# Two scatter tables in place of four in the first layer of a graph network kernel

## The chip, the cores and the metric

The kernel runs on one core of a Trainium2 chip. The metric is the device time of one execution in microseconds (us). Each time below that is not called a median comes from one profiled execution.

## The reference

A graph has 8192 nodes with 128 features each and 262144 edges, sorted by `dst`. Two layers follow each other, and each is added to its input and normalized over the 128 features.

```
def layer0(x, src, dst, weight, W):
    gathered = x[dst] * weight[:, None]
    return segment_sum(gathered, src, 8192) @ W.T
def layer1(x, src, dst, attr, w0..w4):
    summand = tensor_product(x[src], attr, w0..w4)
    return segment_sum(summand, dst, 8192) / sqrt(10)
x = layernorm(x + layer0(x, src, dst, edge_weight, W))
x = layernorm(x + layer1(x, src, dst, edge_attr_9, w0..w4))
```

The change touches only layer 0 and the first norm. In layer 0 the rows that are read lie close together, since `dst` is sorted, but the rows that are added to (`src`) are spread at random over the nodes.

## The kernel before

The program is written by hand for each engine, with semaphores and loops. It has five stages: `setup` (index arithmetic and zero fill), `layer0`, `norm0`, `layer1`, `norm1`. A stage ends with a barrier of all engines, so what one stage gives back is not overlapped by the next.

Layer 0 treats the edges in 2048 tiles of 128 edges, in halves of 8 tiles. For a half, TensorE (PE) fetches the node rows by matmuls with one-hot matrices, ScalarE (ACT) multiplies them by the edge weights into `msg`, PE sums the messages of edges of a tile that have the same `src` (`added`), and ACT copies the sums into one of 16 slots of `sums`, two tiles in a copy (L490). VectorE (DVE) works out the row numbers `row_no` (`rows_of`, L537 to L547). Then GpSimd (POOL) issues one indirect DMA for each tile (L640), which adds 128 rows of 512 bytes to a table in DRAM.

An accumulating DMA reads its rows and writes them later, so two of them on the same table must not overlap. The kernel keeps `TABLES = 4` tables, each with its own semaphore `table_add[k]`, and lets tile t go to table t modulo 4. Before each issue POOL waits until the last DMA on that table has ended, and then tells ACT by the semaphore `turns` that one more slot is free:

```
k = t % TABLES
use = n * (H // TABLES) + t // TABLES
if t == 0:
    pool.wait_ge(rows_known, n + 2)
pool.wait_ge(table_add[k], use * 16 + 16)
pool.sem_inc(turns, 1)
```

The tables are zeroed by `fill` (L178): three in `setup`, the last one after the first windows of `x` have been asked for. `norm0` loads the four tables and `x` in 16 batches of 512 rows (L706, L708); POOL adds the four tables in three adds (L718, L719, L721); PE transposes and multiplies by `W`; DVE and ACT normalize; ACT stores. `norm1` is the same routine without tables.

Of the kernel before, what the change touches and what calls it, by code (L numbers as in the profile page):

```python
# [29 lines left out]
ALU = mybir.AluOpType  # L30
# [11 lines left out]
HALF_TILES = 8  # L42
QUAD_TILES = 4
ROW_EDGES = ROW_TILES * P
TABLES = 4
ZERO_CUTS = 4
EPS = 1e-5
NEIGHBORS = 10.0
# [74 lines left out]
def gnn_kernel(nc, x, src, dst, attr, weight, w_lin, w_tp, consts, out, tables, x1):  # L123
# [8 lines left out]
    with ExitStack() as ctx:  # L132
        def sb(name, shape, dt):
            return ctx.enter_context(nc.sbuf_tensor(name, shape, dt))
# [18 lines left out]
        g.row_start = sb("row_start", [P, g.RN], I32)  # L153
        g.table_add = [ctx.enter_context(nc.semaphore(f"table_add{k}")) for k in range(TABLES)]
        with ExitStack() as mid:
# [5 lines left out]
            setup(nc, g, src, dst, weight, w_lin, consts, tables)  # L161
            layer0(nc, g, x, tables, w_tp)
        norm_stage(nc, g, "norm0", x, x1, tables)
        layer1(nc, g, x1, attr)
        norm_stage(nc, g, "norm1", x1, out, None)

# [7 lines left out]
def fill(pool, g, tables, k):  # L175

    n_zero = (g.N + P) // ZERO_CUTS
    pool.dma_start(tables[k].rearrange("n d -> (n d)").rearrange("(p c f) -> p c f", p=P, c=ZERO_CUTS),  # L178
                   g.acc[:, 0:n_zero].unsqueeze(1).to_broadcast([P, ZERO_CUTS, n_zero])
                   ).then_inc(g.table_add[k], 16)  # L180

def setup(nc, g, src, dst, weight, w_lin, consts, tables):

    RN, TN = g.RN, g.TN
    with ExitStack() as ctx:
# [45 lines left out]
        def _(pool):  # L232
            pool.wait_ge(zeroed, 1)
            for k in range(TABLES - 1):
                fill(pool, g, tables, k)
# [111 lines left out]
def layer0(nc, g, x, tables, w_tp):  # L347
# [4 lines left out]
    with ExitStack() as ctx:  # L352
# [52 lines left out]
        def passes(eng):  # L405

            return eng.Fori(0, eng.value_load(g.n_pass[0:1, 0:1], min_val=1, max_val=g.PASSES0))
# [215 lines left out]
        def _(pool):  # L623
            pool.wait_ge(windows_asked, 1)
            fill(pool, g, tables, TABLES - 1)

            pool.sem_inc(turns, 2 * H - TABLES)
            with passes(pool) as w:
                with pool.Fori(0, RN) as r:  # L630
                    for h in range(2):
                        n = (w * RN + r) * 2 + h
                        for t in range(H):
# [3 lines that stand above are left out]
# [13 lines left out]
SLOTS = 4  # L650

def norm_stage(nc, g, name, x_in, x_out, tables):
# [3 lines left out]
    with ExitStack() as ctx:  # L657
        def sb(n, shape, dt):
            return ctx.enter_context(nc.sbuf_tensor(f"{name}_{n}", shape, dt))

        def sem(n):
            return ctx.enter_context(nc.semaphore(f"{name}_{n}"))
# [3 lines left out]
        tab_t = [[sb(f"t{i}_{k}", [P, BATCH, D], F32) for k in range(n_in - 1)] for i in range(SLOTS)]  # L666
# [11 lines left out]
        loaded = [sem(f"loaded{i}") for i in range(SLOTS)]  # L678
        free = sem("free")
        tab_sum = sem("tab_sum")  # L680
        pool_step = sem("pool_step")
        pre_made = sem("pre_made")
        feat_made = sem("feat_made")
        y_made = sem("y_made")
# [13 lines left out]
        @block.sync  # L698
        def _(sp):
            sp.sem_inc(free, SLOTS)  # L700
            with sp.Fori(0, NB // SLOTS) as i:  # L701
                for s in range(SLOTS):
                    b = i * SLOTS + s
                    sp.wait_ge(free, b + 1)
                    for k in range(n_in - 1):
                        sp.dma_start(tab_t[s][k][:], tiles(tables[k][0:g.N, :])[bass.ds(b, 1)].squeeze(0)  # L706
                                     ).then_inc(loaded[s], 16)
                    sp.dma_start(x_t[s][:], tiles(x_in)[bass.ds(b, 1)].squeeze(0)).then_inc(loaded[s], 16)  # L708

        @block.gpsimd  # L710
        def _(pool):
            if tables:
                assert len(tables) == 4
                with pool.Fori(0, NB // SLOTS) as i:
                    for s in range(SLOTS):
                        t0, t1, t2, t3 = [t[:] for t in tab_t[s]]
                        pool.wait_ge(loaded[s], i * (16 * n_in) + 16 * n_in)
                        nc.gpsimd.tensor_tensor(t0, t0, t1, ALU.add).then_inc(pool_step, 1)  # L718
                        nc.gpsimd.tensor_tensor(t2, t2, t3, ALU.add).then_inc(pool_step, 1)  # L719
                        pool.wait_ge(pool_step, i * (2 * SLOTS) + (2 * s + 2))  # L720
                        nc.gpsimd.tensor_tensor(t0, t0, t2, ALU.add).then_inc(tab_sum, 1)  # L721
            else:
                pool.sem_inc(y_made, 2)
                with pool.Fori(0, NB // 2) as i:
                    for s in range(2):
                        b = i * 2 + s
                        pool.wait_ge(y_made, b + 1)
                        nc.gpsimd.tensor_copy(feat[s][:], g.acc[:, bass.ds(b * (BATCH * P), BATCH * P)].rearrange(
                            "f (p a) -> f a p", a=BATCH)).then_inc(feat_made, 1)
# [367 lines left out]
```

## Time and profile before

| | before |
|---|---|
| median of 3 runs | 7495.48 us (7493.65 to 7499.33) |
| profiled execution, span from first to last instruction | 7497.9 us |
| setup and first windows | 0 to 61.8 us |
| layer 0, first to last scatter-add issue | 61.85 to 3853.23 us |
| norm0 | about 3861 to 3949 us |
| layer 1 | about 3949 to 7437 us |
| norm1 | about 7437 to 7498 us |
| POOL busy over the span | 69% |
| PE busy over the span | 57% |
| mean granted TensorE clock | 0.666 of full speed |

The profiled execution has no time of its own beside its span; the span lies 2.4 us above the median of the runs. In a row of the groups of instructions, the first number behind the bar is busy time in us and the second the mean duration in ns. In a row of the timeline the first number is the start in us and the second how long the row lasts; the bracket tells how long the engine had been idle and what released it. A releaser `issue` means that nothing in the profile was waited for.

### The profile page before, as it was taken

The page shows a single profiled execution, that of the slowest core. Times are in us where ns is not written, and L with a number is a line of the kernel's source. Part 1 is how long each engine was busy: PE and PEld are TensorE (multiplying, and loading weights), DVE is VectorE, ACT ScalarE, POOL GpSimd, SP SyncE. Part 2 cuts the span into 40 slices and gives each one's busy share as a digit, 9 for nine tenths or more (in the row PEclk, how much of TensorE's full clock was granted, in tenths as well). Part 3 has the DMA queues.
Part 4 walks back from the last instruction along what each step waited for, and adds up shares of the span by engine and source line. Part 5 has one row for each costly group of instructions (what it writes and reads, how often), then busy time and mean ns, then how long its engine had stood idle before and what let it go on. Part 6 is the DMA issues. An engine that isn't in the chain of part 4 may idle for free. (4 is left out here: it accounts for less than half of the span.)

```text
span 7497.9 us, 88065 instructions
## 1 busy us (share of the span) xinstructions
PE 4281.0 (57%) x20579; PEld 3387.1 (45%) x20709; DVE 2007.2 (27%) x4415; ACT 1277.5 (17%) x3653; POOL 5183.9 (69%) x4168
## 2 busy tenths in 40 slices
PE   5555555556555555556545556555555665555555
PEld 4444444444444444444434445444444554444444
DVE  4222222222222222222242222222222222222224
ACT  2222222222222222222221000000000000000002
POOL 5888888888888888888875555555555555555554
PEclk7666666666667667666666665766766656676665
DMA  5444444444444444444451111111111111111112
GB/s 137 40 40 40 40 40 40 40 40 40 40 40 40 40 40 40 40 40 40 40 149 47 42 41 41 41 41 41 42 42 42 41 41 41 41 42 42 42 42 69
DMA packets 423293, 349.11 MB, mean 47 GB/s; under 512 B 74464, under 2 KB 369632, under 8 KB 420848
## 3 DMA queue, kind: packets, MB, share of 16 engines
q0 software_dynamic: 362560, 285.74, 27.8%
q1 hardware_dynamic: 56112, 54.84, 2.4%
q10 hardware_dynamic: 4608, 8.39, 0.3%
q14 instruction: 9, 0.07, 0.0%
q8 instruction: 4, 0.07, 0.0%
HBM read 189.03 MB, written 159.65 MB: 47 GB/s over the span
## 5 line engine op out<-in xcount | busy, mean ns | idle before, releaser
L640 POOL DMA_INDIRECT table<-sums,row_no x2048 | 3168.3, 1547 | 637.9 <-issue 491.8
L935 POOL DMA_INDIRECT feat<-x,ids x2048 | 1935.1, 945 | 1549.7 <-PE quad L998 945.9
L469 PE MATMUL added<-msg,same 128*128 128x130 f32 x4096 | 1010.6, 403 | 1545.7 <-ACT sums L490 853.7
L469 PEld LDWEIGHTS added<-msg,same 128*128 128x128 f32 x4096 | 797.5, 280 | 1809.1 <-ACT sums L490 993.9
L998 PE MATMUL quad<-attr_hot,feat 128*128 128x144 f32 x4096 | 996.6, 411 | 1062.8 <-DVE attr_hot L1027 1023.7
L998 PEld LDWEIGHTS quad<-attr_hot,feat 128*128 128x128 f32 x4096 | 844.3, 285 | 1240.3 <-issue 1216.7
L1006 PE MATMUL mixed<-group,mix 128*128 128x192 f32 x2304 | 676.3, 478 | 401.2 <-DVE group L1041 276.2
L490 ACT COPY sums<-added 128x260 f32<-128x260 f32 x1024 | 385.2, 376 | 2811.6 <-POOLq L639 2789.5
L1006 PEld LDWEIGHTS mixed<-group,mix 128*128 128x128 f32 x2304 | 635.2, 299 | 413.4 <-DVE group L1041 284.7
L1027 DVE TENSOR_TENSOR attr_hot<-hot,attr_t 128x1152 f32<-128x1152 f32 x256 | 346.6, 1354 | 1533.1 <-remote 1502.1
L537 DVE TENSOR_SCALAR away<-src_col,cst 128x8 f32 (+1 forms) x256 | 59.2, 231 | 2577.6 <-ACT sums L490 2577.6
L457 PE MATMUL got<-win_s,onehot 128*128 128x128 bf16 x6144 | 690.8, 309 | 4.4 <-DVE onehot L523 3.9
L457 PEld LDWEIGHTS got<-win_s,onehot 128*128 128x128 bf16 x6144 | 664.2, 149 | 21.5 <-issue 5.6
L1041 DVE TENSOR_TENSOR group<-group,quad 128x504 f32 (+1 forms) x512 | 347.7, 679 | 1100.7 <-PE quad L998 528.0
L959 ACT CAST ids<-src_col 128x8 int32 x256 | 50.5, 197 | 3050.8 <-DMA feat<-x,ids 3015.0
L482 ACT ACTIVATE msg<-got,w_col 128x128 f32<-128x128 f32 x2048 | 557.7, 384 | 49.9 <-issue 26.3
L523 DVE TENSOR_SCALAR onehot<-dst_b,node_id 128x1024 bf16<-128x1024 f32 x256 | 327.2, 1278 | 0.0
L525 DVE TENSOR_TENSOR same<-src_b,src_col 128x1024 f32<-128x1024 f32 x256 | 310.7, 1213 | 0.0
L439 PE MATMUL dst_b<-dst_lo,ident_bf 128*128 128x512 bf16 x514 | 257.3, 501 | 23.8 <-issue 19.1
L990 PE MATMUL quad<-zero_bf 1*128 1x504 bf16 x512 | 249.3, 487 | 9.3 <-issue 8.9
L955 ACT ACTIVATE group<-group 128x1728 uint32<-128x1728 uint32 x128 | 210.3, 1643 | 159.7 <-remote 158.6
L439 PE MATMUL src_b<-src_hi,ident_bf 128*128 128x512 bf16 x514 | 211.0, 410 | 0.0
(109 smaller groups left out, 2033.7 us busy)
## 6 DMA issues: line engine op xcount, KB each, us to landing
table<-sums,row_no POOLq DMA_INDIRECT x2048
feat<-x,ids POOLq DMA_INDIRECT x2048
table<-acc POOLq DMA_DIRECT2D x4, 4160.0 KB
win_x<-in_x SPq DMA_DIRECT2D x256, 64.0 KB
norm_t<-table SPq DMA_DIRECT2D x64, 256.0 KB, 4.7
attr_in<-in_edge_attr SPq DMA_DIRECT2D x129, 72.0 KB
norm_x<-in_x SPq DMA_DIRECT2D x16, 256.0 KB, 5.5
x<-norm_z ACTq DMA_DIRECT2D x16, 256.0 KB, 4.5
```

What stands on the lines that cost most here:

```text
L439: last = nc.tensor.matmul(to[:, c * 512:(c + 1) * 512], pick, parts[k][0:RN, cols], start=(k == 0), stop=(k == 1))
L457: last = nc.tensor.matmul(got[:, q, (t % 4) * P:(t % 4 + 1) * P], onehot[h][:, t * P:(t + 1) * P], win_s[h][:, k, :], start=(k == 0), stop ...
L469: last = nc.tensor.matmul(added[:, j % 2, i * R_COLS:(i + 1) * R_COLS], same[h][:, t, :], msg[h][:, t, :], start=True, stop=True)
L482: last = nc.scalar.activation(msg[h][:, t, 0:D], got[:, q, (t % 4) * P:(t % 4 + 1) * P], ACT.Copy, scale=g.w_col[:, bass.ds(r * ROW_TILES ...
L490: nc.scalar.copy(sums[:, h * H + 2 * j:h * H + 2 * j + 2, :], added[:, j % 2, 0:2 * R_COLS].rearrange("p (t c) -> p t c", t=2)).then_inc(s ...
L523: nc.vector.tensor_scalar(onehot[h][:], dst_b[:], node_id[:, own], None, ALU.is_equal).then_inc(onehot_made, 1)
L640: pool.indirect_dma_start(tables[k], bass.IndirectOffsetOnAxis(ap=row_no[:, h * H + t:h * H + t + 1], axis=0), sums[:, h * H + t, 0:D], No ...
L935: pool.indirect_dma_start(feat[:, t, :], None, x1, bass.IndirectOffsetOnAxis(ap=ids[t // H][:, t % H:t % H + 1], axis=0),).then_inc(feat_i ...
L998: nc.tensor.matmul(bank[:, :, bass.ds(off, WIN)], feat[:, t, :], attr_hot[t // H][:, t % H, :, :], start=False, stop=(t % Q == Q - 1), ski ...
L1006: last = nc.tensor.matmul(mixed[:, z, 0:GROUP_WIN], g.mix[:, m, :], group[z][:, m, :], start=(m == 0), stop=(m == NA - 1))
L1027: nc.vector.tensor_tensor(attr_hot[h][:], hot[:].unsqueeze(2).to_broadcast(s4), by_tile[:, h * H:h * H + H, :].unsqueeze(3).to_broadcast(s ...
L1041: nc.vector.tensor_tensor(to, to, quad[:, q, 0:NA * QUAD_WIN].rearrange("p (m n) -> p m n", m=NA), ALU.add).then_inc(quad_added, 1)
```

## The change

`TABLES` becomes 2. So tile t goes to table t modulo 2, and before each scatter-add POOL waits for the DMA two tiles earlier instead of four tiles earlier. `turns` starts at 14 instead of 12. The fill in `setup` writes one table instead of three, and the late fill the second one. `norm0` loads two tables instead of four and has one add on POOL for each batch.

```diff
-TABLES = 4
+TABLES = 2
...
-        pool_step = sem("pool_step")
...
             if tables:
-                assert len(tables) == 4
+                assert len(tables) == 2
                 with pool.Fori(0, NB // SLOTS) as i:
                     for s in range(SLOTS):
-                        t0, t1, t2, t3 = [t[:] for t in tab_t[s]]
+                        t0, t1 = [t[:] for t in tab_t[s]]
                         pool.wait_ge(loaded[s], i * (16 * n_in) + 16 * n_in)
-                        nc.gpsimd.tensor_tensor(t0, t0, t1, ALU.add).then_inc(pool_step, 1)
-                        nc.gpsimd.tensor_tensor(t2, t2, t3, ALU.add).then_inc(pool_step, 1)
-                        pool.wait_ge(pool_step, i * (2 * SLOTS) + (2 * s + 2))
-                        nc.gpsimd.tensor_tensor(t0, t0, t2, ALU.add).then_inc(tab_sum, 1)
+                        nc.gpsimd.tensor_tensor(t0, t0, t1, ALU.add).then_inc(tab_sum, 1)
```

The order on POOL in the loop of layer 0 before, for the first six tiles of a half (`table_add0` is the semaphore of table 0; the `ISA` rows of L638 are register arithmetic for the values that are waited for):

```order
L638 ISA [waits rows_known]
L640 DMA table<-sums,row_no 8320x128 [waits table_add0]
L640 DMA table<-sums,row_no 8320x128 [waits table_add1]
L640 DMA table<-sums,row_no 8320x128 [waits table_add2]
L640 DMA table<-sums,row_no 8320x128 [waits table_add3]
L638 ISA
L640 DMA table<-sums,row_no 8320x128 [waits table_add0]
L640 DMA table<-sums,row_no 8320x128 [waits table_add1]
```

The same place of POOL in the changed kernel:

```order
L638 ISA [waits rows_known]
L640 DMA table<-sums,row_no 8320x128 [waits table_add0]
L640 DMA table<-sums,row_no 8320x128 [waits table_add1]
L638 ISA
L640 DMA table<-sums,row_no 8320x128 [waits table_add0]
L640 DMA table<-sums,row_no 8320x128 [waits table_add1]
L638 ISA
L640 DMA table<-sums,row_no 8320x128 [waits table_add0]
```

The number of scatter-adds stays; between two that wait for the same semaphore there is one other where there were three.

In `norm0`, one batch on POOL before (`norm_t_0` to `norm_t_3` are the tiles loaded from the four tables):

```order
L718 TENSOR_TENSOR norm_t_0<-norm_t_0,norm_t_1 128x512 [waits norm0_loaded0]
L719 TENSOR_TENSOR norm_t_2<-norm_t_2,norm_t_3 128x512
L720 ISA
L721 TENSOR_TENSOR norm_t_0<-norm_t_0,norm_t_2 128x512 [waits norm0_pool_step]
L718 TENSOR_TENSOR norm_t_0<-norm_t_0,norm_t_1 128x512 [waits norm0_loaded1]
```

And two batches in the changed kernel, where each batch is one row:

```order
L717 TENSOR_TENSOR norm_t_0<-norm_t_0,norm_t_1 128x512 [waits norm0_loaded0]
L717 TENSOR_TENSOR norm_t_0<-norm_t_0,norm_t_1 128x512 [waits norm0_loaded1]
```

Two of three adds and the wait between them are gone.

## Rows read from the trace of the kernel before

**Rows 1.** The page: busy times and the costliest group

```profile
span 7497.9 us, 88065 instructions
PE 4281.0 (57%) x20579; PEld 3387.1 (45%) x20709; DVE 2007.2 (27%) x4415; ACT 1277.5 (17%) x3653; POOL 5183.9 (69%) x4168
L640 POOL DMA_INDIRECT table<-sums,row_no x2048 | 3168.3, 1547 | 637.9 <-issue 491.8
```

**Rows 2.** Timeline of POOL in the middle of layer 0

```profile
1999.28 1.54 POOL L640 DMA_INDIRECT table<-sums,row_no  x1 [0.30 <-issue]
2001.12 1.54 POOL L640 DMA_INDIRECT table<-sums,row_no  x1 [0.30 <-DMA table<-sums,row_no]
...
2004.82 1.63 POOL L640 DMA_INDIRECT table<-sums,row_no  x1 [0.30 <-DMA table<-sums,row_no]
```

**Rows 3.** Waits from 2000 to 2100 us (in total, times, longest)

```profile
ACT sums L490 <- POOLq L639: 74.6, 27, 3.5
DVE away L537 <- ACT sums L490: 71.1, 7, 10.3
```

**Rows 4.** Timeline of POOL: first two scatter-adds and the last one

```profile
61.85 1.68 POOL L640 DMA_INDIRECT table<-sums,row_no  x1 [13.33 <-issue]
63.84 1.56 POOL L640 DMA_INDIRECT table<-sums,row_no  x1 [0.30 <-issue]
...
3853.23 1.54 POOL L640 DMA_INDIRECT table<-sums,row_no  x1 [0.30 <-issue]
```

**Rows 5.** When waits for tables passed: L639 in four stretches, L645 once

```profile
L639 POOLq EVENT_SEMAPHORE  x2: 17/17/17, 61.0 to 61.6; - x2
L639 POOLq EVENT_SEMAPHORE  x2: 17/17/17, 62.2 to 62.8; - x2
L639 POOLq EVENT_SEMAPHORE  x2: 17/17/17, 65.3 to 67.2; - x2
L639 POOLq EVENT_SEMAPHORE  x4: 17/17/17, 2002.7 to 2008.1; - x4
L645 POOLq EVENT_SEMAPHORE  x1: 43/43/43, 3856.5 to 3856.5; - x1
```

**Rows 6.** Layer 1: wait of L933 passed, then the next gather starts

```profile
L933 POOLq EVENT_SEMAPHORE  x1: 17/17/17, 5027.6 to 5027.6; - x1
5028.38 0.95 POOL L935 DMA_INDIRECT feat<-x,ids  x1 [7.66 <-PE quad L998]
L933 POOLq EVENT_SEMAPHORE  x1: 17/17/17, 7343.8 to 7343.8; - x1
7344.55 0.95 POOL L935 DMA_INDIRECT feat<-x,ids  x1 [7.70 <-PE quad L998]
```

**Rows 7.** norm0: the stretch (DMA share, GB/s last), first POOL add; L815 in both norms

```profile
3861.00:3949.00 88.00, 41.71 (x192) 33.98 (x192) 52.64 (x192) 39.52 (x97) 59.98 (x48) 0.62 0.82 286
3867.71 1.26 POOL L718 TENSOR_TENSOR norm_t<-norm_t,norm_t 128x512 f32<-128x512 f32 x1 [12.94 <-DMA norm_x<-in_x]
3875.48 0.69 DVE L815 TENSOR_TENSOR norm_z<-norm_x,norm_y 128x512 f32<-128x512 f32 x1 [38.36 <-PE norm_y L748]
3940.45 0.69 DVE L815 TENSOR_TENSOR norm_z<-norm_x,norm_y 128x512 f32<-128x512 f32 x1 [0.96 <-PE norm_y L748]
7440.46 0.69 DVE L815 TENSOR_TENSOR norm_z<-norm_x,norm_y 128x512 f32<-128x512 f32 x1 [3.68 <-DMA norm_x<-x]
7489.02 0.69 DVE L815 TENSOR_TENSOR norm_z<-norm_x,norm_y 128x512 f32<-128x512 f32 x1
```

**Rows 8.** Setup: stretch with the fills (DMA share, GB/s last), then DVE

```profile
3.00:23.00 20.00, 8.37 (x42) 7.51 (x43) 12.18 (x11) 7.08 (x8) 2.45 (x3) 1.00 0.99 392
11.57 1.23 DVE L252 CAST rows_f<-rows_i 128x2048 f32<-128x2048 int32 x1 [3.07 <-DMA rows_i<-in_dst]
42.21 0.15 DVE L292 TENSOR_SCALAR n_pass<-some 128x1 int32<-128x1 f32 x1
```

## The prediction

> **What bounds the kernel now.** I read the page first. POOL is the busiest engine (69%), and its largest group is the scatter-add of layer 0: 2048 DMA_INDIRECT of 1.547 us, with 637.9 us of idle time before them that nothing in the profile explains [rows 1]. Next the timeline of POOL in the middle of layer 0: one scatter-add starts every 1.85 us, 1.54 us of work and 0.30 us between two [rows 2]. The waits of the same stage say that the other engines follow: in 100 us ACT waited 74.6 us at L490 for POOL's queue to free a slot, and DVE 71.1 us for ACT [rows 3]. So layer 0 is as long as POOL's row of issues: from 61.85 to 3853.23 us there are 2047 intervals in 3791.4 us, 1.852 us each [rows 4]. The reader is to see that neither PE nor the data of the DMAs sets this pace; the descriptor writing does.
>
> The question is whether POOL can hold 1.85 us when each scatter-add must wait for the one two tiles before. For that three more durations are needed.
>
> **How long until a scatter-add has landed.** The rows of L639 show when a table's wait passed. The first four passed at 61.0, 61.6, 62.2 and 62.8 us, since those tables had only their zero fill to wait for. The fifth, the first that waits for a scatter-add, passed at 65.3 and the sixth at 67.2 us [rows 5]; the adds they wait for had started at 61.85 and 63.84 us [rows 4], so 3.45 and 3.36 us before. The first two took 1.68 and 1.56 us of POOL instead of 1.54, which explains the surplus. In the middle, the passes from 2002.7 to 2008.1 us [rows 5] belong to the adds that started at 1999.28 and 2004.82 us [rows 2]: 3.42 and 3.28 us. After the last add of all, started at 3853.23 us [rows 4], the final wait (L645) passed at 3856.5 us [rows 5]: 3.27 us, with no add behind it. I take 3.33 us from start to landing seen by POOL.
>
> That also explains why four tables cost nothing. The pass for tile t comes 3.33 us after the start of tile t-4, and the start of tile t is 4 x 1.85 = 7.4 us after that one. The wait is real at POOL's queue but over 4.1 us before the add must start.
>
> **From the released wait to the start of the descriptor work.** With two tables, tile t may pass at 3.33 us after the start of t-2, and at the present pace it would have to start 2 x 1.852 = 3.70 us after it. The slack is 0.37 us. The trace of layer 0 never shows a scatter-add that starts straight after its table wait, except the first: passed at 61.0 us [rows 5], started at 61.85 us [rows 4], 0.85 us, the first use of this instruction. In layer 1, POOL sometimes waits for PE with nothing ahead of it, and there the step is clean: passed 5027.6, started 5028.38; passed 7343.8, started 7344.55 [rows 6]. The passes are rounded to a tenth, so the steps are 0.73 to 0.83 and 0.70 to 0.80 us, and 0.73 to 0.80 fits both. These are gathers with 0.95 us of work, not adds with 1.54 us, but the step lies ahead of that work. I take the middle, 0.77 us. From below I bound it by the spacing of passes at the start, 62.2 to 62.8 us [rows 5]: 0.6 us is what POOL's queue needs to hand on one scatter-add while the descriptor writer is busy with another. From above by the 0.85 us of the first add.
>
> **Sum for the adds.** An add starts 3.33 + 0.77 = 4.10 us after the one two tiles before, which is 2.05 us for each against 1.852. Whether the two chains lie evenly or as 1.85 and 2.25 us makes no difference to the mean. 2047 x 2.05 = 4196 us instead of 3791: **+405 us**. Scatter of the landing times is not won back, since there is no slack left that could absorb it; it is inside the mean of 3.33 us. Bounds: (3.27 + 0.6) / 2 = 1.935 us gives +170 us; (3.42 + 0.85) / 2 = 2.135 us gives +579 us.
>
> Who waits behind POOL? ACT's slot release (`turns`) comes with the pass of the wait. Before, slot release for a tile came with the pass 11 tiles ahead, which lay 4.1 us before that add's start; now with the pass 13 tiles ahead, 0.8 us before its start. Counted in POOL's pace that is about the same place, and ACT has 74.6 us of waiting in 100 [rows 3] as cover. No term.
>
> **Norm0.** Now 15 intervals of L815 run from 3875.48 to 3940.45 us, 4.33 us for each batch, in a stage with a DMA share of 0.82 at 286 GB/s [rows 7]. A batch moves six tiles of 256 KB (four tables, `x`, the store), four after the change: by bytes 4.33 x 4/6 = 2.9 us. Then DVE and ACT come first: norm1, which is the same routine without tables, needs (7489.02 - 7440.46)/15 = 3.24 us [rows 7]. Norm0 has PE's and ACT's extra steps, so I take 3.5 us: 15 x 0.83 = -12.5 us. Before the first batch, two adds of 1.26 us [rows 7] fall away, and two loads of 256 KB, 1.8 us at 286 GB/s: -4.3 us. Together **-17 us**; bounds 0 and -25.
>
> **Zero fill and setup.** POOL issues the three fills between 3 and 23 us, with a DMA share of 0.99; DVE waited 3.07 us for the `dst` rows meanwhile [rows 8]. But the fills stand behind each other in one queue: the first one and the row loads still share the engines as before. The end of setup is DVE's chain (42.21 us) [rows 8], and the late fill, which precedes the first add, stays. No term; if the cover were not what I think, 3.07 us of waiting is the gain. The new second table is filled by the late fill and is needed by tile 1, not tile 3: tile 1's wait passed at 61.6 us, and tile 3's wait for that very fill at 62.8 us without holding up anything, with passes 0.6 us apart [rows 5]. At most 1 us. Layer 1 and norm1 are untouched.
>
> **Total.** 405 - 17 = +388 us on the span of 7497.9 us: 7885.9 us. The span lies 2.4 us above the median, so 7884 us rounded up, 5.2% slower.
>
> **A rule against this.** What the trace has: 1.54 us of writing descriptors [rows 2], then 3.33 - 1.54 = 1.79 us until POOL sees the landing. The Trainium skill ("DMA: Bandwidth & Descriptors", section on the anatomy of one DMA from gpsimd) puts the whole DMA at about 2.0 us plus bytes / 436 GB/s and calls descriptor generation small. Its estimate for 64 KB is 2.15 us: then tile t-2 would always have landed, and two tables would cost nothing; this is the first rival below. The trace disagrees in the part for descriptors, and the measurement decides.
>
> **The rivals.**
>
> - *Hidden landing* (other side: faster). The place is the wait at L639. If the add started within 0.37 us after the pass, or landed so much earlier that the sum of both stayed under 3.70 us, the pace would stay 1.852 us and only norm0 would move: 7495.5 - 17 = 7479 us, faster by 0.23%. For it: DMAs are less crowded with two in flight. Against it: the landing after the last add, with no other behind it, was still 3.27 us, and the step with an idle descriptor writer was 0.73 us or more [rows 6]. It decides from a sum of 3.70 us down; mine is 4.10.
> - *Half hidden*. The step from pass to start overlaps the 1.54 us of the preceding add, since the pass comes about 1.3 us after that add's start. With 0.6 us and 3.3 us: 1.95 us each, +201 us in all, and 7495.5 + 201 - 17 = 7680 us. Against it: 1.28 + 0.6 us is past the end of the preceding work (1.54), so the descriptor writer is idle again, as in [rows 6].
> - *Step of the first add*. Scatter-adds need 0.85 us where gathers need 0.77, and landings lie at 3.42: 2.135 us each, 7495.5 + 579 - 17 = 8058 us. For it: the only scatter-add seen at this step. Against it: it was the first of its kind; its own work took 1.68 instead of 1.54 us.
>
> **How the numbers follow.** Mine 0.80 (its own range 7820 to 7960, which is 3.28 to 3.37 us for the landing and 0.74 to 0.82 for the step); hidden 0.05, half hidden 0.08, step of the first add or worse 0.07. The range of 7780 to 7990 us takes in mine and the near side of the two neighbours. A measurement of this kernel tells about 0.2% (15 us) from no change. Of the hidden case a part ends within it: faster 0.03, same 0.03, slower 0.94.
>
> **What would show it.** In the profile after: L640 still at 1.54 us, but with idle time before it of about 0.5 us (about 1040 us in total, from 637.9), starts 4.1 us apart over two tiles, the pass of L639 3.33 us after the add two tiles before and 0.77 us before its own start, the last add near 4258 us. Norm0 some 17 us shorter, the first add still at about 61.9 us. The prediction is wrong if the step is shorter for adds, if landings come sooner, or if the adds keep their 0.30 us of idle time.

## The result and the profile after

The changed kernel takes 7927.08 us in the median of 4 runs (7916.11 to 7932.07), the kernel before 7495.99 us (7493.65 to 7499.33). The ratio is 1.0577, with a 95% interval of 1.0562 to 1.0592: slower by 431 us. The prediction was 7884 us (7780 to 7990). The profiled execution of the changed kernel has a span of 7914.2 us and is the fastest of the four, while the one of the kernel before (7497.9 us) lies above its median; so the stages add up to 416 us, not 431.

The page after; these lines answer to [rows 1]. POOL worked as long at the adds as before, and the idle time before them grew from 637.9 to 1075.4 us, by 437.5 us.

```profile
span 7914.2 us, 88462 instructions
L640 POOL DMA_INDIRECT table<-sums,row_no x2048 | 3165.6, 1546 | 1075.4 <-issue 969.2
```

The timeline of POOL after, at the same time as [rows 2] and with the first and the last add; then the passes of L639 in the stretches from 1998 to 1999.5, 2000 to 2001.5 and 2002 to 2004 us.

```profile
61.44 1.68 POOL L640 DMA_INDIRECT table<-sums,row_no  x1 [13.17 <-DVE row_no L547]
...
1997.67 1.54 POOL L640 DMA_INDIRECT table<-sums,row_no  x1 [0.63 <-issue]
1999.66 1.54 POOL L640 DMA_INDIRECT table<-sums,row_no  x1 [0.45 <-issue]
2001.71 1.54 POOL L640 DMA_INDIRECT table<-sums,row_no  x1 [0.50 <-issue]
2004.52 1.54 POOL L640 DMA_INDIRECT table<-sums,row_no  x1 [1.26 <-issue]
...
4287.78 1.54 POOL L640 DMA_INDIRECT table<-sums,row_no  x1 [0.39 <-issue]
```

```profile
L639 POOLq EVENT_SEMAPHORE  x1: 17/17/17, 1998.9 to 1998.9; - x1
L639 POOLq EVENT_SEMAPHORE  x1: 17/17/17, 2000.9 to 2000.9; - x1
L639 POOLq EVENT_SEMAPHORE  x1: 17/17/17, 2003.0 to 2003.0; - x1
```

Read the two together. The add of 1997.67 us has landed when the wait passes at 2000.9 (3.23 us), and the add behind that wait starts at 2001.71, 0.8 us later. The next pass, 2003.0, is 3.34 us after 1999.66. It should be followed by a start at 2003.8, but the start is at 2004.52: one of the hiccups of the section on the causes. Over all 2046 adds that wait for another add, the whole trace gives 3.314 us from start to pass in the mean; from pass to start (the step) the median is 0.763 us, and 1776 of 2048 steps are under 0.79 us. The row of adds lasts from 61.44 to 4287.78 us, 2.065 us for each.

The waits from 2000 to 2100 us after, for [rows 3]: ACT still waits 65.9 us in 100 for POOL's queue, so it is nobody else who holds POOL up.

```profile
DVE away L537 <- ACT sums L490: 70.6, 6, 12.6
ACT sums L490 <- POOLq L639: 65.9, 20, 4.4
```

In norm0 the stage and its first POOL add after answer to [rows 7] (columns as there): POOL's work fell from 60.0 to 20.3 us and the DMA share from 0.82 to 0.65. The L811 rows are the first and the last batch (L815 before).

```profile
4295.00:4373.00 78.00, 43.21 (x192) 36.93 (x192) 43.84 (x192) 40.11 (x97) 20.26 (x16) 0.57 0.65 216
4300.16 1.26 POOL L717 TENSOR_TENSOR norm_t<-norm_t,norm_t 128x512 f32<-128x512 f32 x1 [10.84 <-DMA norm_x<-in_x]
4305.38 0.69 DVE L811 TENSOR_TENSOR norm_z<-norm_x,norm_y 128x512 f32<-128x512 f32 x1 [35.28 <-PE norm_y L744]
4364.61 0.69 DVE L811 TENSOR_TENSOR norm_z<-norm_x,norm_y 128x512 f32<-128x512 f32 x1 [0.96 <-PE norm_y L744]
```

The difference of the two spans by stage, each from the first or last rows of the kind named:

| stage | before | after | difference |
|---|---|---|---|
| up to the first add | 61.85 | 61.44 | -0.4 |
| first to last add | 3791.4 | 4226.3 | +434.9 |
| last add to first batch of norm0 | 22.25 | 17.60 | -4.7 |
| first to last batch of norm0 (15 intervals) | 64.97 (4.33 each) | 59.23 (3.95 each) | -5.7 |
| last batch of norm0 to first of norm1 (layer 1) | 3500.0 | 3492.1 | -7.9 |
| rest | | | +0.1 |
| span | 7497.9 | 7914.2 | +416.3 |

### The profile page after: what moved, and what is told of

It is laid out like the page before. It is cut to its first block and busy times, and to the rows that moved or that the text cites. A ratio compares the mean times of both kernels' runs of the same rounds, so it can differ in the third digit from the quotient of the medians.

```text
span 7914.2 us, 88462 instructions
## 1 busy us (share of the span) xinstructions
PE 4348.5 (55%) x20579; PEld 3449.9 (44%) x20709; DVE 2034.7 (26%) x4415; ACT 1278.2 (16%) x3653; POOL 5142.7 (65%) x4134
## 5 line engine op out<-in xcount | busy, mean ns | idle before, releaser
L640 POOL DMA_INDIRECT table<-sums,row_no x2048 | 3165.6, 1546 | 1075.4 <-issue 969.2
L469 PE MATMUL added<-msg,same 128*128 128x130 f32 x4096 | 1063.8, 420 | 1929.6 <-ACT sums L490 1029.0
L469 PEld LDWEIGHTS added<-msg,same 128*128 128x128 f32 x4096 | 844.1, 295 | 2198.6 <-ACT sums L490 1172.9
L994 PE MATMUL quad<-attr_hot,feat 128*128 128x144 f32 x4096 | 1015.3, 417 | 1072.4 <-DVE attr_hot L1023 1044.3
L994 PEld LDWEIGHTS quad<-attr_hot,feat 128*128 128x128 f32 x4096 | 860.3, 290 | 1254.8 <-issue 1224.9
```

Of the source, the lines that this page charges most:

```text
L469: last = nc.tensor.matmul(added[:, j % 2, i * R_COLS:(i + 1) * R_COLS], same[h][:, t, :], msg[h][:, t, :], start=True, stop=True)
L640: pool.indirect_dma_start(tables[k], bass.IndirectOffsetOnAxis(ap=row_no[:, h * H + t:h * H + t + 1], axis=0), sums[:, h * H + t, 0:D], No ...
L994: nc.tensor.matmul(bank[:, :, bass.ds(off, WIN)], feat[:, t, :], attr_hot[t // H][:, t % H, :, :], start=False, stop=(t % Q == Q - 1), ski ...
```

## The experiments

The theory: an add can't start before the landing of the one it waits for (3.31 us after that one's start) plus the step from pass to start (0.76 us). With that add K places back, the pace is the greater of 1.85 and (3.31 + 0.76)/K us; hiccups, single steps of POOL's queue that take longer, come on top where K leaves no slack. The rivals put a part of the loss on the landing (crowded DMAs, the kind of DMA), on the number of tables and the memory they cover, or on the stages around.

The experiments ran on other chips than the first comparison. Three groups of runs of the kernel before, made with them, have medians of 7160, 7125 and 6584 us. The row of adds is alike on all where the waits are hidden: the kernels with undisturbed adds have 3788 to 3790 us there. So each run is compared with the kernel before on its own chip, and its adds by their stage.

**Two tables for the adds alone.** The kernel before, four tables filled and summed.

```diff
-            pool.sem_inc(turns, 2 * H - TABLES)
+            pool.sem_inc(turns, 2 * H - 2)
...
-                            k = t % TABLES
-                            use = n * (H // TABLES) + t // TABLES
+                            k = t % 2
+                            use = n * (H // 2) + t // 2
```

> The kernel before, with four tables filled and summed, but the scatter-adds go to only two of them in turn. Theory (the distance between two adds that wait for each other sets the pace: 3.31 us from start to landing plus 0.76 us from pass to start, over two, plus hiccups of POOL's queue that are no longer hidden): the row of adds takes 4226 us as in the changed kernel, norm0 stays as before, so 7496 + 435 = 7931 us, or the changed kernel's time plus about 10 us. Rival (part of the loss is from the fills, the norm or the smaller memory that is used): nearer to the kernel before than that by more than 20 us.

Measured: 7539.39 against 7160.17 us, ratio 1.0529 (1.05 to 1.0558), 379 us more. The adds last 4178.5 us, 2.041 us each, 390 us more than with four tables on this kind of chip. The row of the adds:

```profile
L640 POOL DMA_INDIRECT table<-sums,row_no x2048 | 3167.3, 1547 | 1026.6 <-issue 1001.2 <-DMA table<-sums,row_no 25.4
```

By the letter of its mark (more than 20 us nearer to the kernel before) the rival would have it, since 379 us is 56 less than the forecast of 435. But the missing part lies in the landing: it is 3.269 us in the mean here, 0.045 us less than in the first comparison, and 0.045/2 x 2047 = 46 us is nearly the whole difference between 4226 and 4178. The shorter landing belongs to the chip and not to the tables: on this chip it is 3.267 us with four tables in turn as well (the trace of the run on norm0 below), where the first chip had 3.322. And the changed kernel itself, run again later on a third chip, has 4181.8 us for its adds, within 4 us of this run with all four tables filled. So the loss is in the adds, and the fills and the norm have no part in it that could be seen.

**All adds to one table.** As before with `k = 0` and a use count of `n * H + t`.

> Four tables filled and summed, all scatter-adds go to one. Theory (landing plus step, nothing else): 3.31 + 0.76 = 4.07 us for each add, 2047 of them 8341 us, plus 50 us of hiccups at full price: 7496 - 3791 + 8391 = about 12100 us. Rival (the landing is long because two adds share the DMA engines, and gets shorter when alone): a landing under 3.1 us, under 11700 us. Hiccups of POOL's queue should come every 59 and every 112 adds as in the changed kernel, with 0.74 and 1.36 us.

Measured: 11627.31 us on a chip where the kernel before takes 7160 us. The total expected was for the first chip and can't be compared; the adds can: 8299.0 us against the 8391 expected, 4.054 us each. Landing 3.266 us, step 0.763 us, sum 4.029; the remaining 0.025 us for each are some 52 us of hiccups, where 50 were expected. The timeline of POOL and two passes (2012 to 2016 and 2018 to 2019 us):

```profile
2011.18 1.54 POOL L640 DMA_INDIRECT table<-sums,row_no  x1 [2.88 <-DMA table<-sums,row_no]
2015.15 1.54 POOL L640 DMA_INDIRECT table<-sums,row_no  x1 [2.43 <-DMA table<-sums,row_no]
2019.10 1.54 POOL L640 DMA_INDIRECT table<-sums,row_no  x1 [2.40 <-DMA table<-sums,row_no]
```

```profile
L639 POOLq EVENT_SEMAPHORE  x1: 17/17/17, 2014.4 to 2014.4; - x1
L639 POOLq EVENT_SEMAPHORE  x1: 17/17/17, 2018.3 to 2018.3; - x1
```

From 2011.18 to 2014.4 an add lands in 3.2 us with no other add under way, no sooner than with another beside it. The rival of the crowded landing falls: under 3.1 us was its mark. The hiccups are there, but every 60 and 113 adds, not 59 and 112.

The packets tell why there was no crowd to thin out. In every trace with accumulating adds of 128 rows, the packets of an add run from 2.12 to 2.9 us after its start (medians), 0.8 us long. Adds start at least 1.84 us apart, so the packets of two adds did not overlap with four tables either.

**Four tables in pairs.** All four in use, in the order 0 1 0 1 2 3 2 3.

```diff
-                            k = t % TABLES
-                            use = n * (H // TABLES) + t // TABLES
+                            k = t % 2 + 2 * (t // 4)
+                            use = n * 2 + (t % 4) // 2
```

`turns` starts at `2 * H - 6`, since fewer adds are known to have ended when a wait passes.

> Four tables, all in use, in the order 0 1 0 1 2 3 2 3 within a half: half of the adds wait for the one two before, half for the one six before. Theory (only the distance counts): of four adds, three start 1.847 us after the one before and one 4.07 - 1.847 = 2.23 us, 1.94 us in the mean, so 7496 + 187 = 7683 us, up to 7710 with hiccups. Rival (the number of tables in use or the memory that they cover sets the landing): no slower than before, 7496 us.

Measured: adds 4012.2 us, 1.960 us each, where 1.943 follows from 1.847 and 4.07 us without hiccups; 224 us more than with four tables in turn. The whole took 7361.79 us in one run against a median of 7160.17, 202 us more, where 187 to 214 were expected. The rhythm in the timeline is the one worked out: one long interval (2.18 us, idle 0.64), then three of about 1.85.

```profile
2005.79 1.54 POOL L640 DMA_INDIRECT table<-sums,row_no  x1 [0.30 <-issue]
2007.97 1.54 POOL L640 DMA_INDIRECT table<-sums,row_no  x1 [0.64 <-issue]
2009.85 1.54 POOL L640 DMA_INDIRECT table<-sums,row_no  x1 [0.34 <-issue]
2011.69 1.54 POOL L640 DMA_INDIRECT table<-sums,row_no  x1 [0.30 <-issue]
2013.54 1.54 POOL L640 DMA_INDIRECT table<-sums,row_no  x1 [0.31 <-issue]
2015.77 1.54 POOL L640 DMA_INDIRECT table<-sums,row_no  x1 [0.68 <-issue]
```

Four tables don't help where the wait reaches only two adds back. It is the distance, not the number of tables in use.

**Norm0 over two tables alone.** The kernel before with `norm_stage(nc, g, "norm0", x, x1, tables[0:2])` and the single add of the changed kernel.

> The kernel before with its adds over four tables, but norm0 loads and sums only tables 0 and 1 (the sums of the other two are left out of the result). Theory: norm0 is worth what the two traces show, 22.25 to 17.6 us before the first L815 and 4.33 to 3.95 us for each batch: 7496 - 10 = 7486 us (ratio 0.9986). Rival (norm0 gains as predicted): 7479 us. Rival (the gain of norm0 in the changed kernel is from something else there): 7496 us.

Measured: ratio 0.9984 (0.9967 to 1.0001), which holds both theory and both rivals; by the clock the run is inconclusive. Its trace isn't. The last add and the first and last L812 of norm0:

```profile
3848.75 1.54 POOL L640 DMA_INDIRECT table<-sums,row_no  x1 [0.30 <-issue]
3866.56 0.69 DVE L812 TENSOR_TENSOR norm_z<-norm_x,norm_y 128x512 f32<-128x512 f32 x1 [33.90 <-PE norm_y L745]
3925.98 0.69 DVE L812 TENSOR_TENSOR norm_z<-norm_x,norm_y 128x512 f32<-128x512 f32 x1 [0.97 <-PE norm_y L745]
```

17.8 us and 59.4 us, as in the changed kernel (17.6 and 59.2), against 22.25 and 64.97 on the first chip: 10.0 us less. On this run's own chip three traces have a norm0 of four tables, with 84.6, 84.9 and 86.4 us for the two parts together against 77.2 here; by them norm0 gives 7 to 9 us. The adds took 3787.9 us, as before.

**Half of the rows.** The changed kernel, each add with partitions 0 to 63 only; the other half of every tile's sums is left out.

```diff
-  tables[k], bass.IndirectOffsetOnAxis(ap=row_no[:, h * H + t:h * H + t + 1], axis=0),
-  sums[:, h * H + t, 0:D], None, compute_op=ALU.add)
+  tables[k], bass.IndirectOffsetOnAxis(ap=row_no[0:64, h * H + t:h * H + t + 1], axis=0),
+  sums[0:64, h * H + t, 0:D], None, compute_op=ALU.add)
```

> The changed kernel with each scatter-add of only partitions 0 to 63 (half of the rows of every tile are left out of the sums). Two tables. Theory on the landing: writing descriptors gets shorter (about 0.8 to 1.1 us instead of 1.54), the data phase by some 0.4 us, so landing 2.3 to 2.7 us and a pace of 1.55 to 1.75 us: 7200 us or less. Theory on the hiccups: the ones every 59 adds come when a ring of descriptors is used up, so their distance grows to 105 to 118 adds; those every 112 adds stay. Rival on the hiccups: they belong to the number of instructions, and stay at 59.

Measured: 7228.7 us against 7124.89, so 104 us more than the kernel before, where the forecast (7200 us or less against 7496) was nearly 300 us less; adds 3918.6 us, 1.914 us each. The sizes missed: writing descriptors takes 1.41 us for 64 rows, hardly less than 1.54 for 128, and the landing is 3.02 us, not 2.3 to 2.7. Even with half of the rows, two tables are slower than four with all. The pace is again (3.015 + 0.761)/2 = 1.888 plus 0.026 of hiccups. Of the hiccups, those every 59 adds are gone, and a series every 127 adds (at 126, 253, 380, 507, ...) has come, with a step of 2.30 us: 1.54 us more than usual, twice the 0.74 of the first series. Those every 112 (at 106, 218, 330, ...) are where they were in the changed kernel. So the first kind depends on the rows in an add, and the second doesn't. The rival (59 as before) falls, and the forecast of 105 to 118 was too low.

**Writing instead of adding.** The changed kernel without `compute_op`; what several tiles have for one row is overwritten, not summed.

```diff
-  sums[:, h * H + t, 0:D], None, compute_op=ALU.add)
+  sums[:, h * H + t, 0:D], None)
```

> The changed kernel with scatters that overwrite instead of adding (the sums of a row that several tiles share are left out). Theory (the landing is writing descriptors plus the fixed way of a DMA, whatever it does with the data): landing 3.1 to 3.3 us, pace 2.0 us or a little less, 7800 to 7927 us. Rival (reading the old rows makes the landing long): landing under 2.9 us, and the wait for two before costs nothing: pace 1.85 us, near 7490 us.

```profile
1998.52 0.96 POOL L640 DMA_INDIRECT table<-sums,row_no  x1 [0.74 <-issue]
1999.87 0.96 POOL L640 DMA_INDIRECT table<-sums,row_no  x1 [0.39 <-issue]
```

Measured: 6470.33 us against 7124.89. The theory on the landing fell, and further than the rival had it. Writing descriptors takes 0.96 us instead of 1.54, and the landing is 2.26 us in the median, so 1.30 us behind the descriptors instead of 1.77. Accumulation costs twice: 0.58 us of POOL and 0.47 us on the way.

The packets show where the 0.47 us lie. These are the DMAs of POOL's queue for one add: with accumulation from 2013.2 to 2014.2 us of the run over one table (the add of 2011.18 us), and without from 2000.0 to 2000.6 us here (the one of 1998.52 us).

```profile
q0 software_dynamic: 144, 0.07, 71.4%
q0 software_dynamic: 32, 0.07, 33.9%
```

16 packets of each are the semaphore's. The data goes in 128 packets of 512 bytes with accumulation and in 16 of 4096 bytes without, and the packets last 0.78 against 0.34 us (medians over the row of adds). The other two parts are the same: 0.58 us from the last descriptor to the first packet, and 0.37 us from the end of the last packet to the pass. The pace of 1.85 us of the rival did not appear either, since the work that set it got shorter as well: (2.26 + 0.78)/2 = 1.52 us was the wait, 1.544 the measured pace. Short and long intervals alternate, 1.31 and 1.73 us in the median; the shortest is 1.26 us, which POOL's work of 0.96 and 0.30 between two sets. Of the hiccups, none comes every 59 adds; every 112 the step is 3.5 us in place of 0.78, twice the usual surplus. So 128 rows alone don't make the first kind.

**Three tables.** Adds in strict turn of three, three fills, norm0 with three loads and two adds. POOL's loop runs over three rows of edges (48 adds) and the last two rows follow it.

```diff
-TABLES = 4
+TABLES = 3
...
+            uses = [len(range(k, RN * ROW_TILES, TABLES)) for k in range(TABLES)]
...
+                with pool.Fori(0, RN // ROWS) as i:
+                    rows(w, i * ROWS, i, ROWS)
+                rows(w, RN // ROWS * ROWS, RN // ROWS, RN % ROWS)
...
-                        nc.gpsimd.tensor_tensor(t2, t2, t3, ALU.add).then_inc(pool_step, 1)
```

> Three tables everywhere: adds in strict turn of three, two fills in setup and the late one, norm0 loads three tables and has two adds on POOL. Theory (an add may start 4.07 us after the one it waits for, and with three tables that one lies 5.54 us back): 1.47 us of slack hides also the hiccups of up to 1.36 us, the adds keep 1.852 us, norm0 gives about 5 us: 7491 us, ratio 0.9993, same. Rival (hiccups or late landings come through): adds above 1.86 us, slower than before by 10 us or more.

Measured: 7104.18 against 7124.89 us, ratio 0.9972 (0.9956 to 0.9988). The adds took 3790.3 us, 1.852 each: neither the landings nor the hiccups come through. But 0.28% is more than norm0 can give, so the kernel ran again with the changed kernel beside it.

> The kernel with three tables once more, since its first ratio, 0.9972 [0.9956, 0.9988], is larger than what its trace explains. Theory (adds as before, norm0 shorter by 10 us as with two tables, the rest of the first ratio was scatter of layer 1): ratio 0.9986, interval with 0.9986 in it. Rival (three tables also help elsewhere): again 0.9975 or lower.

> The changed kernel without any edit, for its ratio on the same chip as three tables. Theory (the added time lies in the adds and doesn't depend on how long layer 1 takes): landing 3.27 to 3.32 us, adds 4178 to 4226 us, norm0 10 us shorter, so 380 to 425 us above the kernel before on this chip. Rival (the loss is a share of the whole time, or layer 1 takes part): outside that.

```profile
L637 POOL DMA_INDIRECT table<-sums,row_no x2048 | 3165.0, 1545 | 637.6 <-issue 612.6 <-DMA table<-sums,row_no 25.0
```

Measured: three tables 6575.02 against 6584.36 us, ratio 0.9986 (0.9977 to 0.9995), faster by 9 us; adds 3787.9 us, and the idle time before them (the row above) is that of [rows 1]. The changed kernel 6964.95 us, 381 us above the kernel before, at the lower end of what was expected; ratio 1.0576 (1.056 to 1.0593); adds 4181.8 us. Layer 1 took about 2583 us in both traces, 900 less than on the first chip, and the loss in the adds is the same. From last add to last batch, norm0 took 83.0 us with three tables here and 76.8 us in the run before, 76.3 with two in this group and 84.6 to 87.2 with four (in the traces of two other chips). So the gain of norm0 with three tables is between 2 and 10 us, as far as traces of different chips can be compared. Three tables beat both kernels, the one with four by 0.1 to 0.3% only.

## Why the prediction was right, point by point

*The bound*: right. POOL's row of issues sets layer 0, and ACT and DVE wait for it in both kernels.

*Landing, 3.33 us*: right, 3.314 measured in the changed kernel. It was read off the passes of a wait that cost nothing before.

*Step, 0.77 us*: right, 0.763. The gathers of layer 1 (0.77) gave the price of a step that the adds had shown only once, at the very first; that add's 0.85 us was too high, and the overlap of the second rival (0.6 us) isn't there: no step of the changed kernel is under 0.76 us.

*The sum for the adds, +405 us*: a term is missing. By the measured durations (3.314 + 0.763)/2 x 2047 = 4173 us, 381 more than before; the trace has 4226. The 54 us between are steps that take longer, most of them hiccups: at 34 adds, each 59 after the last, the step is 1.50 instead of 0.76 us, and at 18, each 112 after the last, it is 2.12 us. Together that is 34 x 0.74 + 18 x 1.36 = 50 us. With two chains of adds one could expect half of it, but the add behind a late one starts no sooner than 1.85 us after it and is late too: the adds right behind have 40 us more between them. (50 + 40)/2 = 45 us of the 54 are these two series with their followers; the other 9 are single late steps that were not sorted. Two of the first kind and one of the second, in passes and starts of the changed kernel:

```profile
L639 POOLq EVENT_SEMAPHORE  x1: 17/17/17, 298.5 to 298.5; - x1
300.01 1.54 POOL L640 DMA_INDIRECT table<-sums,row_no  x1 [1.33 <-issue]
L639 POOLq EVENT_SEMAPHORE  x1: 17/17/17, 419.5 to 419.5; - x1
420.98 1.54 POOL L640 DMA_INDIRECT table<-sums,row_no  x1 [1.18 <-issue]
L639 POOLq EVENT_SEMAPHORE  x1: 17/17/17, 509.4 to 509.4; - x1
511.55 1.54 POOL L640 DMA_INDIRECT table<-sums,row_no  x1 [1.81 <-DMA table<-sums,row_no]
```

The steps are 1.5, 1.5 and 2.1 us; 121 us lie between the first two starts, 59 adds. The prediction took the step for a constant. Between pass and start the kernel before can't show otherwise, since over 4 us lie there. But its trace does hold the hiccups, one instruction further on: behind every fourth pass POOL's queue comes to register arithmetic (L638, or L630 at the end of a row of 16 tiles). It gets there 0.54 us after the pass usually (the first two lines), 1.26 us at every 228th add and 1.88 us at every 220th (the next two pairs).

```profile
L639 POOLq EVENT_SEMAPHORE  x1: 17/17/17, 441.0 to 441.0; - x1
L630 POOLq ALU_OP  x1: 32/32/32, 441.5 to 441.5; - x1
L639 POOLq EVENT_SEMAPHORE  x1: 17/17/17, 470.7 to 470.7; - x1
L630 POOLq ALU_OP  x1: 32/32/32, 472.0 to 472.0; - x1
L639 POOLq EVENT_SEMAPHORE  x1: 17/17/17, 648.4 to 648.4; - x1
L630 POOLq ALU_OP  x1: 32/32/32, 650.3 to 650.3; - x1
```

Those surpluses, 0.72 and 1.34 us, are within 0.02 us those of the two hiccups, and four tables hid them. So the missing term stood in the trace that the prediction was made from. The phrase "Scatter of the landing times is not won back [...] it is inside the mean" was right for the landings and silent on the steps.

*Norm0, -17 us*: right in sign, mis-sized: -10.4 in the two traces, and -7 to -10 with norm0 changed alone. Before the first batch -4.7 (forecast -4.3); but each batch took 3.95 us, not 3.5. DMA is no longer the bound (share 0.65), and POOL is idle two thirds of the time; DVE waits for PE (L744) before nearly every batch, and PE for ACT's copy. What bounds that ring was not taken apart.

*Zero fill, 0*: right, the first add starts 0.4 us earlier.

*The rule on the length of a DMA*: the Trainium skill ("DMA: Bandwidth & Descriptors", section on the anatomy of one DMA from gpsimd) would have had add t-2 land in time by its 2.0 us and bytes. Here the landing is 3.31 us, and still 3.27 for an add with no other under way. The same section of the Trainium skill puts most of the fixed cost at the receipt of the write in the target memory. The traces here don't show it so: of 3.27 us, 1.54 are descriptors, 0.58 lie before the first packet, 0.78 are packets and 0.37 come after them. Whether a packet's recorded time contains a part of the receipt, they don't tell.

In sum: 405 became 435 in the adds (-24 by the two durations, +54 by hiccups), -17 became -10, and layer 1 gave 8 us. No experiment explains that; on one chip of the experiments layer 1 took anything from 3122 to 3167 us in four traces, so it may be scatter. The profiled run is the lowest of four, 11 us under the median; why is open.

The range was drawn for doubts about landing and step, and knew nothing of hiccups. That it held them is luck in part: the two durations had been 24 us too high. The inner range of 7820 to 7960 us doesn't follow from the durations beside it either; 3.28 to 3.37 and 0.74 to 0.82 us give 7802 to 7976.

## What to carry to other kernels

Where buffers take turns behind a completion, one round over all of them must be longer than completion plus the step from pass to start plus the occasional hiccup of the queue: here 3.31 + 0.76 + 1.36 = 5.43 us, against 3.69 us for a round of two and 5.54 for one of three. A wait that costs nothing still shows its landing time in the passes of the queue, and the instruction behind it shows the hiccups, so the price of a shorter round can be read before anything is built. Take the smallest number of buffers that keeps slack (three here), not the one that saves the most work elsewhere.

## What the runs showed of the hardware that was not expected

- POOL's queue has hiccups between pass and start. With two tables, 0.74 us more every 59 scatter-adds of 128 rows (1.54 us more every 127 of 64 rows, none without accumulation) and 1.36 us more every 112 (2.7 without accumulation). Unhidden they cost 45 to 50 us of 4226.
- The distance of the first kind is 60, 59 and 58 adds with one, two and three tables in turn, that of the second 113 and 112 with one and two. With four only every fourth add can be read, and the distances of 228 and 220 fit 57 and 110. So each further table in turn makes them one shorter. A store of descriptors that is used up would look like this, for the first kind; it was not shown, and what the other counts is open.
- Accumulation costs POOL 0.58 us for each indirect DMA of 128 rows (1.54 against 0.96) and another 0.47 us on the way. Half of the rows save only 0.13 us of POOL.
- An accumulating DMA with no other under way lands no sooner (3.27 us) than with others around it (3.27 to 3.32).
- Layer 1, the same code, took 3492 to 3500, 3113 to 3168 and 2583 to 2585 us on the chips of this study, while the row of adds with hidden waits stayed within 4 us. Not looked into.
- POOL's part that reads the queue ran more than two adds ahead: with four tables, a wait passed 4.1 us before its add started. A version in which the add itself waits, without the small instruction that also frees the slot, was not tried.
